# A router that keeps token blocks stationary and moves its weight columns, with five edits beside it, in a decoder layer on one core

## The reference, cut to what matters

```python
shared = jax.nn.silu(x @ Ws_gate) * (x @ Ws_up) @ Ws_down        # 704 hidden
scores = jax.nn.softmax(x @ W_router, axis=-1)                   # W_router: 512 x 8
topk_vals, topk_idx = jax.lax.top_k(scores, 2)
...
h = jax.nn.silu(xf @ We_gate[e]) * (xf @ We_up[e])               # 8 experts, 352 hidden
routed = sum over the two chosen experts of weight * (h @ We_down[e])
x = _layernorm(x + routed + shared)
```

## Time and profile before

| | |
|---|---|
| median of 3 runs | 1147.04 us (1146.91 to 1148.95) |
| the profiled execution | 1147.71 us, its span 1145.7 us |
| mean granted clock over the span | 0.97 |
| TensorE busy | 1073.2 us (94%), 6790 products |
| VectorE busy | 689.6 us (60%) |
| ScalarE busy | 457.5 us (40%) |
| GpSimd busy | 278.6 us (24%) |
| HBM | 156 GB/s over the span |

### The profile page before, as it was taken

The page is one execution under the profiler, slowest core; times in us unless marked ns, Lnnn a source line. Parts: engine busy times, 40 slices in busy tenths (PEclk is TensorE's granted clock), DMA queues, the critical chain, the costliest instruction groups (busy, mean ns, idle before and its releaser), DMA issues. The chain is left out here.

```text
span 1145.7 us, 19191 instructions
## 1 busy us (share of the span) xinstructions
PE 1073.2 (94%) x6790; PEld 904.8 (79%) x6790; DVE 689.6 (60%) x1522; ACT 457.5 (40%) x810; POOL 278.6 (24%) x367
## 2 busy tenths in 40 slices
PE   7999999999779999999689889999999999899996
PEld 6688888888668888877468579998999999777784
DVE  4836465474266777765346467777777776253475
ACT  5614324154126445544252155555555554221210
POOL 4510100121313333333252022222222220313030
PEclk9999999999868999999989889999999999999999
DMA  5403040215687788882260277677666774524141
GB/s 168 164 1 110 0 192 0 69 42 176 162 219 204 200 233 239 223 217 72 80 234 14 95 249 240 232 247 238 228 224 229 237 224 156 176 64 144 40 160 60
DMA packets 91140, 179.35 MB, mean 157 GB/s; under 512 B 8176, under 2 KB 38128, under 8 KB 89296
## 3 DMA queue, kind: packets, MB, share of 16 engines
q1 hardware_dynamic: 84416, 155.06, 43.3%
q0 software_dynamic: 6672, 23.60, 6.3%
HBM read 136.95 MB, written 41.42 MB: 156 GB/s over the span
## 5 line engine op out<-in xcount | busy, mean ns | idle before, releaser
L45 PE MATMUL e_ps_h<-e_x_lo,e_gu_hi 128*128 128x256 f32 (+1 forms) x552 | 155.9, 282 | 5.0 <-DVE e_x_lo L1943 5.0
L46 PE MATMUL e_ps_h<-e_x_hi,e_gu_lo 128*128 128x256 f32 (+1 forms) x552 | 153.9, 279 | 0.0
L47 PE MATMUL e_ps_h<-e_x_hi,e_gu_hi 128*128 128x256 f32 (+1 forms) x552 | 153.7, 279 | 0.0
L45 PE MATMUL a_ps_proj<-a_x_lo,arena 128*128 128x512 f32 x272 | 108.9, 400 | 9.6 <-DVE a_x_lo L357 6.9
L938 DVE CUSTOM_DVE_ANT_0 b_dump<-b_ps_s,b_mask 128x128 f32<-128x128 f32 (+1 forms) x256 | 80.3, 354 | 53.1 <-PE b_ps_s L1118 51.3
L46 PE MATMUL a_ps_proj<-a_x_hi,arena 128*128 128x512 f32 x272 | 108.4, 398 | 0.0
L47 PE MATMUL a_ps_proj<-a_x_hi,arena 128*128 128x512 f32 x272 | 108.2, 398 | 0.0
L45 PEld LDWEIGHTS e_ps_h<-e_x_lo,e_gu_hi 128*128 128x128 f32 (+1 forms) x552 | 99.5, 180 | 6.2 <-DVE e_gu_lo L1947 5.2
L46 PEld LDWEIGHTS e_ps_h<-e_x_hi,e_gu_lo 128*128 128x128 f32 (+1 forms) x552 | 99.6, 180 | 1.0
L47 PEld LDWEIGHTS e_ps_h<-e_x_hi,e_gu_hi 128*128 128x128 f32 (+1 forms) x552 | 99.5, 180 | 0.0
L376 DVE SCALAR_TENSOR_TENSOR a_xc<-a_ps_proj,a_taps,a_xc 128x510 f32<-128x510 f32 (+2 forms) x96 | 71.7, 747 | 45.5 <-ACT a_xc L316 43.2
(11 more groups left out here) (323 smaller groups left out, 2643.0 us busy)
## 6 DMA issues: line engine op xcount, KB each, us to landing
f_gate_up_raw<-we_gate_up SPq DMA_DIRECT2D x88, 352.0 KB, 5.3
b_sk<-qk_split SPq DMA_DIRECT2D x48, 256.0 KB, 4.5
b_sq<-qk_split SPq DMA_DIRECT2D x48, 256.0 KB, 5.9
qk_split<-arena SPq DMA_DIRECT2D x24, 512.0 KB, 6.1
f_down_raw<-we_down SPq DMA_DIRECT2D x23, 512.0 KB, 3.9
y_slots<-f_y_tile SPq DMA_DIRECT2D x23, 512.0 KB, 2.8
f_x_next<-x SPq DMA_DIRECT2D x7, 1024.0 KB, 6.8
f_down_raw<-we_down SPq DMA_DIRECT2D x23, 192.0 KB, 4.0
```

The costliest lines, as they stand in the source:

```text
L45: pe.matmul(out, a_hi, b_lo, start=first, stop=False)
L46: pe.matmul(out, a_lo, b_hi, start=False, stop=False)
L47: return pe.matmul(out, a_hi, b_hi, start=False, stop=last)
```

## The change

1. Router products. The stationary operand is now a block of 128 tokens of x (`x_hi` or `x_lo`), the moving one the 16 columns `w_hi_lo` (8 of hi, 8 of lo). For each chunk that is 8 pairs of a weight load and a product of 16 columns, in place of 3 products of 512. All logits gather by token in one PSUM bank over the whole router; the copies to `lg_t` and the 16 transposes are gone. VectorE adds the two halves (two small operations).
2. The last group is transposed straight out of `kept`, once it is normalized, and not loaded again.
3. VectorE's order at the start of `route`: two rests, `w_lo`, the small operations of the layer norm, two rests, the four normalizations. The four `bn_stats` moved to the end of `cross_attention`.
4. The weight parts are rounded at other places (`PARTS_AT`), and the first hidden unit waits for them chunk by chunk instead of for all four ahead of it.
5. At the end of `cross_attention` VectorE makes `a_lo` of the last batch, not GpSimd.
6. The fifth `up` goes ahead of `hot_lo`; the table of tokens is made before the third output tile, not the fourth.
7. `experts` splits x after the first weight chunk, not after the fourth.
8. `combine` normalizes the last group in two parts, three tiles and then one.

The diff, with little of its context:

```diff
--- before.py
+++ after.py
@@ -780,8 +780,6 @@
...
                     pool.tensor_tensor(bln.rstd[:], bln.var[:], bln.power[:], ALU.pow).then_inc(rstd_done, 1)
-            for u in range(2):
-                rest(B - 1, u)
...
@@ -1033,8 +1031,16 @@
...
                 normalize(B - 1, u)
+            for u in range(2):
+                dve.wait_ge(a_hi_done, 2 * (B - 1) + u + 1)
+                cs = slice(UC * u, UC * u + UC)
+                dve.tensor_tensor(a_lo[:, cs], a_raw[:, cs], a_hi[:, cs].bitcast(F32), ALU.subtract).then_inc(a_lo_done, 1)
+            for k in range(BT):
+                dve.bn_stats(ln.stats[:, k], res[:, k])
             for k in range(BT):
                 add(B - 1, k)
+                dve.wait_ge(out_added, 2 * (B - 1) + k + 1)
+                dve.bn_stats(ln.stats[:, BT + k], res[:, BT + k])
...
@@ -1346,7 +1352,7 @@
...
-    def hidden(self, pe, n, u, x_done=None):
+    def hidden(self, pe, n, u, x_done=None, w_done=None):
...
@@ -1357,6 +1363,8 @@
...
                     pe.wait_ge(self.x_lo_done, self.BANKS + DC * x_done + c + 1)
+                if w_done is not None and s == 0:
+                    pe.wait_ge(w_done, c + 1)
                 mm = three_pass(pe, self.ps_h[:, u % 2, s], self.gu_hi[:, c, at], self.gu_lo[:, c, at],
...
@@ -1412,9 +1420,9 @@
...
         w_raw = sb("w_raw", [P, DC, E_N])
-        w_hi = sb("w_hi", [P, DC, P], F32R)
-        w_lo = sb("w_lo", [P, DC, P], F32R)
-        lg_t = sb("lg_t", [E_N, T])
+        w_hi_lo = sb("w_hi_lo", [P, DC, P], F32R)
+        from_lo = sb("from_lo", [P, NT, E_N])
+        raw_lg = sb("raw_lg", [P, NT, E_N])
         int_a = sb("int_a", [P, 2 * P], I32)
...
@@ -1448,11 +1456,11 @@
...
-        ps_l = shared.ps_out
         ps_r = shared.ps_x[:, 1]
         each_e = NT * E_N
-        ps_logits, ps_prior, ps_total = (ps_r[:, k * each_e:(k + 1) * each_e] for k in range(3))
-        ps_token = ps_r[:, 3 * each_e:3 * each_e + NB]
+        ps_logits = shared.ps_out[:, 0, 0:2 * each_e].rearrange("p (t k e) -> p t k e", k=2, e=E_N)
+        ps_prior, ps_total = (ps_r[:, k * each_e:(k + 1) * each_e] for k in range(2))
+        ps_token = ps_r[:, 2 * each_e:2 * each_e + NB]
         parts = shared.parts(w_gate_up, w_down)
...
@@ -1475,8 +1483,6 @@
...
         lg_chunk = sem("lg_chunk")
-        lg_read = sem("lg_read")
-        turned = sem("turned")
         sub_both_done = sem("sub_both_done")
...
@@ -1484,9 +1490,9 @@
...
-        CONSTS = 8
-
-        PARTS_AT = {(1, 1): 0, (1, 3): 1, (3, 0): 2, (3, 2): 3}
+        CONSTS = 7
+
+        PARTS_AT = {(1, 1): 0, (2, 0): 1, (3, 1): 2, (3, 3): 3}
         LAST = GROUPS - 1
...
@@ -1511,14 +1517,13 @@
...
             sp.dma_start(x2_dram[LAST], kept[:]).then_inc(x2_stored, 16)
-            for g in range(2, GROUPS):
+            for g in range(2, LAST):
                 sp.wait_ge(shared.x_ready, DC * (g - 1))
-                if g == LAST:
-                    sp.wait_ge(x2_stored, 16)
                 load(g)
...
+            sp.wait_ge(x2_stored, 16)
             sp.wait_ge(part_lo_done, S_PARTS)
...
@@ -1527,15 +1532,14 @@
...
         def _(pool):
+            pool.memset(w_hi_lo[:].bitcast(F32), 0.0).then_inc(consts, 1)
             pool.memset(before[:], 1.0).then_inc(consts, 1)
             pool.memset(ones[:], 1.0).then_inc(consts, 1)
-            pool.memset(w_hi[:].bitcast(F32), 0.0).then_inc(consts, 1)
-            pool.memset(w_lo[:].bitcast(F32), 0.0).then_inc(consts, 1)
             pool.memset(keep[:], 1.0).then_inc(consts, 1)
...
             pool.tensor_tensor(ln.rstd[:], ln.var[:], ln.power[:], ALU.pow).then_inc(rstd_done, 1)
-            pool.wait_ge(consts, 6)
+            pool.wait_ge(consts, 5)
             pool.affine_select(out=before[:], in_=before[:], compare_op=ALU.is_gt, fill=0.0, base=0,
...
@@ -1582,17 +1586,12 @@
...
                     shared.x_round(act, g, c)
-                    if g == 0 and c == 2:
+                    if g == 0 and c == 1:
                         act.wait_ge(w_loaded, 16)
-                        act.wait_ge(consts, CONSTS)
-                        act.activation(w_hi[:, :, 0:E_N], w_raw[:], ACT.Copy).then_inc(w_hi_done, 1)
-                    if g and c == 1:
-                        act.wait_ge(lg_chunk, DC * g)
-                        act.activation(lg_t[:, (g - 1) * GT:g * GT], ps_l[0:E_N, (g - 1) % 2], ACT.Copy).then_inc(lg_read, 1)
+                        act.wait_ge(consts, 1)
+                        act.activation(w_hi_lo[:, :, 0:E_N], w_raw[:], ACT.Copy).then_inc(w_hi_done, 1)
                     if (g, c) in PARTS_AT:
                         split_part(PARTS_AT[g, c])
-            act.wait_ge(lg_chunk, DC * GROUPS)
-            act.activation(lg_t[:, LAST * GT:T], ps_l[0:E_N, LAST % 2], ACT.Copy).then_inc(lg_read, 1)
             act.wait_ge(sub_both_done, 1)
...
@@ -1612,19 +1611,19 @@
...
             shared.begin(dve)
-            for k in range(TILES):
-                moments_step(dve, sums, ln, k, ln_step, 0, var_done)
+            shared.x_rest(dve, 0, 0)
+            shared.x_rest(dve, 0, 1)
+            dve.wait_ge(w_hi_done, 1)
+            dve.tensor_tensor(w_hi_lo[:, :, E_N:2 * E_N], w_raw[:], w_hi_lo[:, :, 0:E_N].bitcast(F32), ALU.subtract)\
+                .then_inc(w_lo_done, 1)
             for k in range(TILES, TILES + 3):
-                moments_step(dve, sums, ln, k, ln_step, 0, var_done)
-                shared.x_rest(dve, 0, k - TILES)
+                moments_step(dve, sums, ln, k, ln_step, -TILES, var_done)
+            shared.x_rest(dve, 0, 2)
+            shared.x_rest(dve, 0, 3)
             dve.wait_ge(rstd_done, 1)
...
                                   ALU.subtract, ALU.mult).then_inc(x2_ready, 1)
-            dve.wait_ge(w_hi_done, 1)
-            dve.tensor_tensor(w_lo[:, :, 0:E_N], w_raw[:], w_hi[:, :, 0:E_N].bitcast(F32), ALU.subtract)\
-                .then_inc(w_lo_done, 1)
-            shared.x_rest(dve, 0, DC - 1)
             dve.memset(raw[1][E_UNITS[2]:P, 2], 0.0).then_inc(pad_expert_known, 1)
...
@@ -1636,10 +1635,11 @@
...
             dve.wait_ge(iotas, 10)
-            dve.wait_ge(turned, 1)
-            logits = ps_logits.rearrange("p (t e) -> p t e", e=E_N)
-            link(dve.tensor_reduce(top[:], logits, AX_X, ALU.max))
-            dve.tensor_tensor(lg[:], logits, each(top[:]), ALU.subtract).then_inc(sub_both_done, 1)
+            dve.wait_ge(lg_chunk, DC * GROUPS)
+            link(dve.tensor_copy(from_lo[:], ps_logits[:, :, 1]))
+            link(dve.tensor_tensor(raw_lg[:], ps_logits[:, :, 0], from_lo[:], ALU.add))
+            link(dve.tensor_reduce(top[:], raw_lg[:], AX_X, ALU.max))
+            dve.tensor_tensor(lg[:], raw_lg[:], each(top[:]), ALU.subtract).then_inc(sub_both_done, 1)
             dve.wait_ge(exp_done, 1)
...
@@ -1698,8 +1698,8 @@
...
+            shared.up(dve, 0, 4)
             link(dve.tensor_tensor(hot_lo[:], repeat(col128[:], P), spread(part_f[:, 1], P), ALU.is_equal))
-            shared.up(dve, 0, 4)
             shared.up(dve, 0, 5)
...
@@ -1707,20 +1707,22 @@
...
             dve.wait_ge(x2_stored, 16)
-            for t in range(TILES - 1):
+            for t in range(TILES):
+                if t == TILES - 2:
+                    dve.wait_ge(placed, 1)
+                    dve.tensor_copy(rt.token_of[:], ps_token).then_inc(token_known, 1)
                 shared.add(dve, kept, 0, t)
-            dve.wait_ge(placed, 1)
-            dve.tensor_copy(rt.token_of[:], ps_token).then_inc(token_known, 1)
-            shared.add(dve, kept, 0, TILES - 1)
...
                 g, c = n // DC, n % DC
-                if g and c == 0:
+                if 0 < g < LAST and c == 0:
                     pe.wait_ge(loaded[g % 2], 16 * ((g + 1) // 2))
-                shared.turn(pe, xt[g % 2], ident, g, c)
+                if g == LAST and c == 0:
+                    pe.wait_ge(x2_ready, TILES)
+                shared.turn(pe, kept if g == LAST else xt[g % 2], ident, g, c)
...
@@ -1731,17 +1733,15 @@
...
                     pe.wait_ge(w_lo_done, 1)
-                if c == 0 and g >= 2:
-                    pe.wait_ge(lg_read, g - 1)
-                three_pass(pe, ps_l[:, g % 2], w_hi[:, c], w_lo[:, c], shared.x_hi[:, c], shared.x_lo[:, c],
-                           c == 0, c == DC - 1).then_inc(lg_chunk, 1)
-            pe.wait_ge(lg_read, GROUPS)
-            for t in range(NT):
-                mm = pe.transpose(ps_logits[:, t * E_N:(t + 1) * E_N], lg_t[:, t * P:(t + 1) * P], ident[0:E_N, 0:E_N])
-            mm.then_inc(turned, 1)
-            pe.wait_ge(part_lo_done, DC)
+                for t in range(TILES):
+                    to = ps_logits[:, TILES * g + t].rearrange("p k e -> p (k e)")
+                    rows = slice(t * P, (t + 1) * P)
+                    pe.matmul(to, shared.x_hi[:, c, rows], w_hi_lo[:, c, 0:2 * E_N], start=n == 0 and t == 0, stop=False)
```

(37 more changed lines are left out.)

## The result

The changed kernel takes 1152.72 us (median of 9 runs, 1148.83 to 1155.94), the kernel before beside it 1147.82 (9 runs, 1145.8 to 1152.42). The ratio is 1.0040, 95% interval 1.0022 to 1.0058: slower, by 0.4 per cent. The forecast was 1144.0 with a range of 1140.5 to 1147.5, so it was wrong, in sign too; what came is the slower rival, a pair at the price of a transpose.

What follows compares the result with a forecast made beforehand. TensorE was to bound the router at 1.2 GHz, with waits at the seams bound row by row. Terms -0.6 + 0.8 + 0 - 0.6 - 0.9 - 1.75 = -3.05 gave a median of 1144.0 us, range 1140.5 to 1147.5.

Steps and rivals of the forecast that it cites:

- the slower rival: Router: a pair costs a transpose's 0.21 us, loads not pulled ahead; +10, so 1154; decides from about 0.18; chance 0.10.
- The bound and the clock: Router: TensorE is the bound from group 2's landing on; granted clock 0.5, 1.2 GHz, for the whole router.
- the price of a pair: Router: a weight load with 16 moving columns costs 0.06 to 0.12 us at the low clock, taken as 0.11.
- The router's term: Block's start to shared expert's first product: 32.4 against 31.6 us, +0.8, bounds -1.7 and +2.4.
- The load of group 2: Router, SyncE's queue: issued behind the last group's store, it lands at 584.1, bounds 582.5 and 585.
- the lead of the start is spent at this load: Router's start: the first product runs four microseconds sooner, but waiting for group 2's load uses that up.
- The seams: Edits at pauses outside the router: 3.85 us gained in all; a rival gave half, 1145.9, chance 0.15.
- Cross-attention's end: VectorE's split and four moved `bn_stats` at the last projection: -0.6, bounds +0.1 and -1.4.
- From the shared expert to the experts: Down projection 0, bounds -2.2 to 0; end of `route` gains 0.6 by the earlier gather.
- The experts' start: Start of `experts`, x split after the first weight chunk: -0.9, bounds -0.6 and -1.3.
- The end of `combine`: Last layer norm in two parts, last store alone: gain 1.75, bounds 1.3 and 2.0; last addition 0.3 late.
- The chances: Whole kernel: faster 0.57, within what can be told from no change 0.32, slower 0.10 plus 0.01 of the seams.

Runs made afterwards that it cites:

- e7_forms: Kernel before plus three groups of 32 unused operations between shared-expert units: fp32r pairs with 16-column blocks, plain fp32 pairs, small transposes; 1159.90 us.
- e4_half_again: Changed kernel without the products of the low parts of x, 4 pairs a chunk instead of 8; 1143.26 us, ratio 0.9958.
- e5_move64: Changed kernel with 64 columns moving in each router pair instead of 16, the other 48 zeros; 1152.11 us, ratio 1.0036.
- e1_wide3: Changed kernel with three wide router products a chunk and the weight-rounding places as before, other edits kept; 1145.55 us, ratio 0.9982.
- e9_seams: Kernel before with only the edits outside the router, whose start and last-group reload stay as before; 1140.47 us, ratio 0.9946.
- e6_wide2_early: Changed kernel with two wide router products a chunk and group 2's load issued ahead of the last group's store; 1140.63 us, ratio 0.9921.
- e1_wide2: Changed kernel with two wide router products a chunk, both weight parts in one stationary block; 1145.09 us, ratio 0.9967.
- e8_turned_early: Changed kernel with group 2's load issued ahead of the store of the normalized last group; 1154.75 us, ratio 1.0054.

## Why the prediction was wrong

**The bound and the clock** were right: 1.2 GHz from the first pair to the last, TensorE busy without a gap, a transpose at 0.21.

**The failed step is the price of a pair.** "At the low clock a pair of 16 columns should cost between 0.06 and 0.12" was taken from the 16 small transposes. It costs 0.21. The halved clock was the right factor, on the wrong row: a small transpose costs about half of a product with as many columns in its block (0.06 and 0.11 at 2.4 GHz). The trace of before had a nearer row, in a stretch whose sums I had quoted: short products at the low clock. Its timeline:

```profile
331.32 0.41 PE L1118 MATMUL b_ps_s<-b_sk,b_sq 96*128 96x128 f32 x1
...
331.54 0.52 PE L1118 MATMUL b_ps_s<-b_sk,b_sq 96*128 96x256 f32 x1
```

A product with 128 columns in its block and 128 moving takes 0.22 there until the next one starts. The start of a single product is a weak price (the one ahead of it, with as many columns, takes 0.10), but the weight loads of the same place are a good one:

```profile
331.22 0.54 PEld L1118 LDWEIGHTS b_ps_s<-b_sk,b_sq 96*128 96x128 f32 x2
331.64 0.55 PEld L1142 LDWEIGHTS b_ps_x<-b_sq,b_sk 98*128 98x128 f32 x2
332.07 0.54 PEld L1118 LDWEIGHTS b_ps_s<-b_sk,b_sq 96*128 96x128 f32 x2
...
331.00:334.00 3.00, 3.00 (x14) 2.90 (x14) 1.80 (x10) 1.47 (x3) 0.98 (x3) 0.50 0.95 369
```

Four loads of blocks of 128 columns start between 331.22 and 332.07, one every 0.21, and PEld is busy 2.90 of 3.00 us: the price of the pairs stood in the trace of before. The transposes of the earlier trace rows, whose blocks have 128 columns too, had the same 0.21. With it the bounds would have been 0.06 to 0.21, the point of 0.18 from which the slower rival decides would have lain inside of them, and 0.10 was too small a chance for that rival.

The Trainium skill ("TensorE: Matmul & The Clock Gate", LDWEIGHTS) gives a load as its columns over 1.2 GHz whatever its rows, 107 ns for 128 columns. I had set that aside because of the pairs of 0.06, which are transposes. For products at 2.4 GHz the runs agree with it on two counts: 0.11 with 128 columns, and the same with 8 rows. For 16 columns the page's formula gives 0.013, an estimate, and a pair takes 0.027 in e7_forms, so there the agreement isn't shown. At 1.2 GHz they don't agree: 0.21.

**The router's term** was +0.8 and came out as +9.12. 128 pairs at 0.21 instead of 0.105 are 13 us more of TensorE, and idle time absorbs some 4 of them: in e4_half_again 3.55 for group 2, which it shows, and 0.65 ahead of an earlier turn. The rival had this sum nearly: "8 us more after chunk 8, and 4.8 more before it, where some 3 of idle time absorb a part", 1154 against 1152.7. Its reason does not hold: it had the loads not pulled ahead under short products, but with 48 more moving columns the chunk stays at 2.48 (e5_move64), so the products run under the loads, and the load alone has the price. Its boundary of 0.18 lies between what was run: with a chunk as of pairs at 0.10 the kernel is faster than before, with 0.21 slower. The sum has a slip besides: from the block's start at 567.04 to 599.7 it is 32.7 and not 32.4, so the term should read +1.1; it changes nothing here.

**The load of group 2** was right to 0.1 us: forecast 584.1, landed 584.2. That "the lead of the start is spent at this load" is shown by e1_wide3 (4.00 of waiting) and by the order turned round (0.52). What I priced as a lost gain is worse than that: e1_wide3 has the seams of e9_seams and the early `w_lo`, and is slower than e9_seams (ratios 0.9982 and 0.9946), because of the wait and of two stretches at the low clock, one from the wait on and one in the first hidden unit. With three products the early load takes all of it away. That the wait also brings the second stretch, 16 us behind it, isn't shown: the kernel before has the low clock at that place too (0.50 from 598.90 to 602.20), where TensorE waited 0.96 for group 2. The store and its queue I saw; the clock beside the wait I did not price.

**The seams** gave more than forecast. Cross-attention's end: -0.6 forecast; A is 0.90 shorter and the wait ahead of it fell from 2.31 to 1.70, so -1.5, just past the bound of -1.4 that I had for a clock that doesn't fall. In e6_wide2_early and e1_wide2 it fell there, and A was 10.4 long; so both bounds are real. From the shared expert to the experts: -0.6 forecast, -1.46 in C, within the bounds of the two steps in it. But C is not a fixed gain: in the changed kernel's trace the low clock in the down projection lasts from 648.20 to 651.50, before from 636.40 to 643.20, and in e8_turned_early, which has the same code there, from 649.50 to 656.20, and its C is 60.17, longer than before. The experts' start: -0.9 forecast, D -1.59; the first product comes 3.63 after the first transpose instead of 6.04, so 2.4 were won there and 0.8 given back. The end of `combine`: -1.75 forecast, E -2.64. The last addition was not late (4.64 behind the third, 4.58 before), addition to normalization took 2.92 and not 3.43, as the root of one column is shorter (0.55 against 1.01 us on GpSimd), and the lone store landed faster. In this trace the seams gave 7.2 together, nearly twice the forecast's 3.85; e9_seams measures 6.2 for them, with 4.1 to 8.3 as its interval.

**The chances.** 0.11 for slower rested on a price taken from a row of another kind. With half of the pairs, so with a chunk of the length forecast, the kernel is faster than before and the time lies in the range; the direction hung on this price alone, the size also on seams that gave more.

## What to carry to other kernels

A matmul with few moving columns is priced by the load of its stationary block: take that price from a row of the same kind (product or transpose) and type, with as many columns in the block, at the same granted clock, and if there is none, take the distance between the weight loads themselves, or let the next longer product of that kind be the upper end. Turning operands so that the narrow matrix moves makes such loads out of wide products: here 48 products of 512 columns, 0.23 each at 2.4 GHz, became 128 loads at 0.21. And when a stage starts earlier, look on the queue for the transfer that the start does not carry along: here one load moved ahead of one store took the ratio from 0.9982 to 0.9910, 8 us.

## What was not expected of the hardware

With few columns moving, a pair at 2.4 GHz costs 0.11 us with 128 columns in its block and 0.03 with 16; its rows (8 or 128) and its moving columns (16 or 64) make no difference. A transpose of 8 or 16 rows through a block of 128 columns costs 0.06. At 1.2 GHz the pair with 128 columns is 0.21 and the small transpose 0.11. A product in f16 with 128 columns in its block costs 0.03 at 2.4 GHz. A product in plain fp32 with 16 columns moving is two instructions of 0.11 each, where one in fp32r is one.
